# Expert part written out one expert ahead, shared part with its down projection inside the next chunk's gate-up

## The reference

```
attention:  pair[i,j] = relu(W2 relu(h_i - h_j + b1) + b2);  sim[i,j] = W3 pair[i,j] + b3, 0 on the diagonal
            for each token the 25 rows of largest sim, softmax over them in 32 heads of width 2, times Wout
mixture:    router -> 2 of 8 experts per token, capacity 1280 slots per expert
            expert:  h = silu(x Wgate) * (x Wup), width 176;  y = h Wdown
            shared:  the same shape on all tokens, width 704
```

## Time and profile before

| | us |
|---|---|
| three runs | 1804.5, 1806.66, 1807.19 (median 1806.66) |
| the profiled execution, own time | 1801.61 |
| its span in the profile | 1799.9 |
| stage 3, first gate-up to last down | 1325.0 to 1561.9 |
| stage 4, first product to the end | 1563.0 to 1799.9 |

### The profile page before, as it was taken

The page is one execution under the profiler, slowest core; times in us unless marked ns, Lnnn a source line. Parts: engine busy times, 40 slices in busy tenths (PEclk is TensorE's granted clock), DMA queues, the critical chain, the costliest instruction groups (busy, mean ns, idle before and its releaser), DMA issues.

```text
span 1799.9 us, 33525 instructions
## 1 busy us (share of the span) xinstructions
PE 1658.4 (92%) x9092; PEld 739.2 (41%) x9092; DVE 1514.7 (84%) x4279; ACT 1457.7 (81%) x2723; POOL 1121.8 (62%) x1045
## 2 busy tenths in 40 slices
PE   6989999999999999999999999999976878899897
PEld 5732222222222222222222222222246877877776
DVE  5876789999999999999999999999967675555555
ACT  4689999999999999999999999999965555423131
POOL 2203467777777777777777777776655501666564
PEclk9999999999999999999999999999988998999998
DMA  4511111121211212122111211111154533212131
GB/s 135 202 51 59 40 40 52 56 57 49 56 49 57 57 50 57 48 58 57 49 57 48 58 53 53 52 47 41 44 167 130 150 100 118 85 55 91 49 93 58
DMA packets 74726, 127.22 MB, mean 71 GB/s; under 512 B 21824, under 2 KB 43200, under 8 KB 74688
## 3 DMA queue, kind: packets, MB, share of 16 engines
q0 software_dynamic: 31744, 69.27, 14.0%
q1 hardware_dynamic: 42944, 57.53, 9.8%
HBM read 86.85 MB, written 35.65 MB: 68 GB/s over the span
## 4 chain that ended last, share of the span: by engine, by line
ACT 52%; issue 14%; PE 13%; DVE 10%; POOL 3%; DMA 1%; ACTq 1%; DVEq 0%; POOLq 0%
ACT arena L967 31%; ACT arena L980 18%; PE ps L809 7%; PE ps L768 4%; POOL arena L679 3%; ACT arena L984 1%; DVE hTe_low L1419 1%; DVE hTs_low L1488 1%; PE ps L779 1%; DMA arena<-slot_outputs,ysidx 1%; DVE xTe_low L1407 1%; DVE arena L1413 1%; ACT hTe_high L1051 1%; DVE arena L1326 1%; DVE arena L1256 1%
## 5 line engine op out<-in xcount | busy, mean ns | idle before, releaser
L615 POOL DMA_INDIRECT arena<-kv_rows,gidx x800 | 848.7, 1061 | 319.3 <-issue 226.3
L768 PE MATMUL ps<-arena,w2t 128*64 128x512 f32 x4096 | 946.8, 600 | 21.9 <-ACT arena L980 8.3
L967 ACT ACTIVATE arena<-arena 128x256 f32<-128x256 f32 x1696 | 804.7, 651 | 1.9 <-DVE arena L1246 1.9
L1256 DVE TENSOR_SCALAR arena<-arena 128x256 f32<-128x256 f32 x2400 | 746.0, 370 | 23.0 <-PE ps L768 20.7
L980 ACT ACTIVATE arena<-ps,b 128x1024 f32<-128x1024 f32 x512 | 639.7, 1250 | 5.5 <-PE ps L768 5.4
L768 PEld LDWEIGHTS ps<-arena,w2t 128*64 128x64 f32 x4096 | 273.3, 136 | 682.8 <-issue 577.1
L779 PE MATMUL ps<-arena,w3win 128*32 128x512 f32 x2048 | 272.8, 605 | 10.5 <-DVE arena L1267 10.3
L1092 ACT ACTIVATE arena<-ps 128x512 f32<-128x512 f32 x40 | 24.0, 599 | 152.9 <-PE ps L809 152.9
L779 PEld LDWEIGHTS ps<-arena,w3win 128*32 128x32 f32 x2048 | 40.3, 108 | 220.0 <-issue 180.1
L601 POOL DMA_INDIRECT slot_inputs<-xstage,istage x64 | 76.1, 1189 | 87.3 <-issue 70.4
L809 PE MATMUL ps<-xTe_high,wug_high 128*112 128x256 f32 (+1 forms) x240 | 77.5, 323 | 54.3 <-DVE xTe_low L1407 54.2
(11 more groups left out here) (144 smaller groups left out, 2020.3 us busy)
## 6 DMA issues: line engine op xcount, KB each, us to landing
arena<-kv_rows,gidx POOLq DMA_INDIRECT x800
slot_inputs<-arena SPq DMA_DIRECT2D x16, 640.0 KB, 3.9
arena<-slot_inputs SPq DMA_DIRECT2D x40, 256.0 KB, 3.2
slot_outputs<-arena SPq DMA_DIRECT2D x40, 256.0 KB, 2.1
xn<-in_L_attn_x_dram SPq DMA_DIRECT2D x16, 256.0 KB, 2.9
xstage<-xn SPq DMA_DIRECT2D x16, 256.0 KB
arena<-in_L_attn_x_dram SPq DMA_DIRECT2D x8, 512.0 KB, 3.8
out_dram<-arena SPq DMA_DIRECT2D x8, 512.0 KB, 4.6
```

What stands on the lines that cost most here:

```text
L615: pool.indirect_dma_start(out=kvg[:, h, r, :], out_offset=None, in_=kv_dram, in_offset=bass.IndirectOffsetOnAxis(ap=gidx[:, h, r:r + 1], a ...
L768: last = nc.tensor.matmul(ps_l2(s)[v * G2:(v + 1) * G2, u, :], w2t[:, :], r1[:, s % R1, 4 * u + 2 * v:4 * u + 2 * v + 2, :], start=True, s ...
L967: last = nc.scalar.activation(r1[:, s % R1, k, :], hneg_now, ACT.Relu, bias=hb_now[:, at:at + 1])
L1256: row = nc.vector.tensor_scalar(r1[:, s % R1, k, :], hneg_now, hb_now[:, at:at + 1], 0.0, ALU.add, ALU.max)
```

## The change

- **Expert part written out.** All 40 groups stand one after the other on every engine, numbered g = 0 to 39. `AHEAD = 2`: transposing and splitting of the slots run two groups ahead, across pairs, with three buffers for their halves.
- **The start.** SP loads the first expert's weights and slots when batch 15 has been copied out of the arena, not at the pair loop's end. POOL splits expert 0 between the gathers of tile 28 and those of tile 29, in the last batch of the pair loop. Slots 0 and 1 are transposed ahead of the last `layer3`, into banks 7 and 4. The loads of expert 1 and of the shared weights follow.
- **Weights.** ACT makes the high halves of expert e (1 to 5) one group ahead of DVE's low halves. POOL splits experts 0, 6 and 7.
- **Left-over attention.** Its pieces are spread over groups 0 to 35 in eight steps instead of five for each tile; POOL paces the last gathers by `gu_done`.
- **Shared part.** Written out, 8 chunks. While PE makes gate and up of chunk c, four down units of chunk c-1 follow each m. Two buffers for the tokens' halves, the activations' halves and the gathered outputs; the residual and the result keep one. The copies of queries and slot numbers (L674, L675) go. DVE weighs tiles 0 and 1 of chunk c-1 behind m = 3 and 4, tiles 2 and 3 behind the last m, and adds the residual in one instruction.

```diff
+    AHEAD = 2
-        xTe_r = [halves(f"xTe{i}", DC * 256, DC, 256) for i in range(2)]
+        xTe_r = [halves(f"xTe{i}", DC * 256, DC, 256) for i in range(AHEAD + 1)]
...
-        WEIGHTS_AT = {(0, 2): 1, (0, 8): 2, (1, 3): 3, (1, 8): 4, (2, 3): 5}
+        HIGH_AT = {2: 1, 7: 2, 12: 3, 17: 4, 22: 5}
+        LOW_AT = {3: 1, 8: 2, 13: 3, 18: 4, 23: 5}
+        ON_POOL = (0, 6, 7)
-        EXP_GROUP = {(0, 8): NT - 3, (1, 6): NT - 2, (2, 5): NT - 1}
+        EXP_GROUP = {11: NT - 3, 22: NT - 2, 31: NT - 1}
...
 # SP
-            sp.wait_ge(r1_dve, NB * BSTEPS)
-            sp.wait_ge(r1_act, NB * BSTEPS)
+            sp.wait_ge(batch_copied, 2 * NB)
...
 # POOL
                 for h in range(HALVES):
+                    if b == NB - 2 and h:
+                        wait_alone(pool, "pool", gathered[0], (b + 1) * (16 * TOPK))
+                        split_expert(0)
                     gather_tile(b, h, False, TOPK if b < NB - 2 else LAST_PACED[h] if b == NB - 2 else 0)
...
+            def gather_outputs(c):
+                if c >= 2:
+                    pool.wait_ge(comb_step, START + (c - 1) * CS)
+            def add_residual(c):
                 pool.wait_ge(resid_loaded, c * 16 + 16)
+            split_tokens(0)
+            split_tokens(1)
+            for c in range(NCH):
+                gather_outputs(c)
+                add_residual(c)
+                if c + 2 < NCH:
+                    split_tokens(c + 2)
...
 # PE
+            for g in range(AHEAD):
+                transpose_slots(g)
+            layer3(NB * BSTEPS, BSTEPS - 1)
+            for g in range(ALL):
+                if g + AHEAD < ALL:
+                    transpose_slots(g + AHEAD)
+                gate_up(g)
+                if g >= BEHIND:
+                    down(g - BEHIND)
...
+            for c in range(NCH):
+                for m in range(SM):
+                    if m == JC:
+                        transpose_heads(c)
+                    shared_gate_up(c, m)
+                    if c:
+                        shared_down(c - 1, UNITS[CT * m:CT * (m + 1)])
+            shared_down(NCH - 1, UNITS)
...
 # DVE
+            def expert_group(g):
+                if g + AHEAD < ALL:
+                    slots_low(g + AHEAD)
+                gate_times_up(g)
+                activations_low(g)
+                if g in LOW_AT:
+                    weights_low(LOW_AT[g])
+                if g in TOPK_AT:
+                    last_topk(*TOPK_AT[g])
+                if g in ATTENTION_AT:
+                    last_attention(*ATTENTION_AT[g])
...
+            OUTPUT_AT = {3: 0, 4: 1}
                     if m:
                         low(m - 1)
+                    if c and m in OUTPUT_AT:
+                        for k in range(2):
+                            weigh_output(c - 1, OUTPUT_AT[m], k)
                 low(JC)
+                if c:
+                    for n in range(2, CT):
+                        for k in range(2):
+                            weigh_output(c - 1, n, k)
+                    add_resid(c - 1)
```

More of the change, by code:

```diff
@@ L379, in lsn_attention_moe_block @@
         GATHER_AT = 9
-        CS = 3 * CT
+        CS = 2 * CT + 1
+        SM = JC + 1
+        UNITS = [(n, m) for n in range(CT) for m in range(SM)]
         GROUPS = BSTEPS // 2
@@ L493, in load_weights, with load_slots, store_group @@
                   .then_inc(we_loaded, 16)
[L495 to L514, removed]
+            def load_slots(g):
+                sp.dma_start(xe[g % GPE], expert_rows(slot_dram, g)).then_inc(xe_loaded[g % GPE], 16)
+            def store_group(g):
+                sp.wait_ge(down_copied, g + 1)
+                sp.dma_start(expert_rows(yslot_dram, g), oute[g % 2]).then_inc(y_stored[g % 2], 16)
             load_weights(0)
@@ L851, in down @@
                         last = products(ps_down(g)[:, n, :], [h[rows, m, n * P:(n + 1) * P] for h in hTe_r[g % 2]],
-                                        [h[rows, m, :] for h in wdn_r[i]], m == 0, m == 1)
+                                        [h[rows, m, :] for h in wdn_r[i % 2]], m == 0, m == 1)
                 last.then_inc(down_done, 1)
-            def expert_pair(j, first):
-                transpose_slots(j, 0, first)
-                for g in range(GB):
-                    if g < GB - 1:
-                        transpose_slots(j, g + 1, first)
-                    gate_up(j, g, first)
-                    if not (first and g < BEHIND):
-                        down(j, g - BEHIND, first)
@@ new lines, in shared_gate_up @@
+            def shared_gate_up(c, m):
+                if m == 0:
+                    pe.wait_ge(xT_split, c * 2 + 2)
+                if m >= 2 and m < JC:
+                    pe.wait_ge(smul_done, c * SM + (m - 1))
+                elif c and m == JC:
+                    pe.wait_ge(smul_done, c * SM)
+                elif c:
+                    pe.wait_ge(smul_done, c * SM - (1 + m))
+                for bank, at in ((2 * (m % 2), m * P), (2 * (m % 2) + 1, (JC + m) * P)) if m < JC else ((5, 2 * JC * P),):
+                    for k in range(DC):
+                        last = products(ps[:, bank, :], [w[:, k, at:at + P] for w in swug_r], [x[:, k, :] for x in xT_r[c % 2]],
+                                        k == 0, k == DC - 1)
+                last.then_inc(sgu_done, 1)
@@ new lines, in transpose_heads, with shared_down @@
+            def transpose_heads(c):
+                wait_alone(pe, "pe", aoT_low, START + c)
+                for n in range(CT):
+                    last = nc.tensor.transpose(ps[0:KD, 4, n * P:(n + 1) * P], qao[:, c * CT + n, :], ident[:, :])
+                last.then_inc(aoT_done, 1)
+            def shared_down(c, units):
+                for n, m in units:
+                    if n == 0:
+                        pe.wait_ge(slow_done, c * SM + (m + 1))
+                    if n == 0 and m == JC:
+                        pe.wait_ge(aoT_low, START + c + 1)
+                    if c and m == 0 and n % 2 == 0:
+                        pe.wait_ge(comb_step, START + (c - 1) * CS + (2 * n + 3))
+                    last = products(ps[:, 6 + n // 2, (n % 2) * D:(n % 2 + 1) * D], [h[:, m, n * P:(n + 1) * P] for h in hTs_r[c % 2]],
+                                    [w[:, m, :] for w in swdn_r], m == 0, m == JC)
```

435 lines of the change are left out of this document (201 added, 234 removed).

## The result

| | before | after |
|---|---|---|
| median of the runs of one comparison | 1805.58 us (4 runs, 1803.63 to 1807.19) | 1757.41 us (4 runs, 1753.95 to 1758.3) |
| ratio, 95% interval | 1 | 0.973 [0.9713, 0.9748] |
| profiled execution, own time / span | 1801.61 / 1799.9 us | 1753.95 / 1752.2 us |
| PE busy, granted clock from the first shared product on | 208.6 of 236.9 us, 0.94 | 196.1 of 210.35 us, 0.97 |

Forecast: 1754. Measured: 1757.41, 48.2 us less than before where 52 were forecast.

A forecast was written before the change was run, and what follows sets the result against it. No engine is full in the two later stages; DVE's own work and waits bound the expert groups, PE's work and waits the shared part. +2 - 4.2 - 16.8 - 33.0 = -52.0 us, forecast 1754 us, range 1742 to 1766.

The forecast's parts named there:

- three waits at pair ends: Expert part: DVE's waits of 4.48, 4.17 and 3.70 us, with no gate-up made ahead; all 12.4 us should go.
- rival B: Shared part: DVE and POOL bound it, period 24.2 to 28 us; at 27, +20 us, 1774; chance 0.13.
- A: Expert part: only its start gains, DVE bounds the groups and other waits replace pair ends; 1771 us; chance 0.14.
- Rival D: PE's written-out code: instruction fetch can't keep up, so the kernel is slower, 1817 at 1.3 us per group or chunk; chance 0.04.
- Part 1: Pair loop's last batch: splitting expert 0 on POOL costs +2 us, bounds 0 to +5.
- Part 3: The forty expert groups: DVE's floor of 189.3 us stays, waits change; last low half 19.0 us earlier, -16.8 for the groups.
- Exponentials: Expert groups 11, 22 and 31: DVE waits for ACT behind its table changes, 10.4 us in all against 9.7 before.
- The hand-over: From the groups' last low half to the first shared product: forecast 0 change.
- So it is just hidden: End of the expert part: POOL's later shared split, 15.7 + 3.8 us, fits in some 24 us; cover 4 us.
- Part 4, chunk 0: Shared part's first chunk, without down products: 15.5 us.
- 4 us of slack per m: Shared part: multiply m is needed only for gate-up m + 2, 5.6 us later, so DVE may be 4 us late.
- Part 4, the tail: From the last gate-up to the end: +20.5 us, the single-buffered residual last, its POOL additions ending at +15.7.

The follow-up runs named there:

- e6: The changed kernel with two more copies and subtractions on POOL directly ahead of expert 0's split: 1760.73 us, ratio 0.976 to the kernel before.
- e7: The changed kernel with own last-chunk residual and result buffers, expert 5's weights one group earlier, chunk 0's residual additions held back: 1747.37 us, ratio 0.9678.
- e10: The same kernel as e7, run again in another comparison as partner of e8: 1747.56 us, ratio 0.9685 to the kernel before.
- e4: The changed kernel with separate buffers for the last chunk's residual and result: 1752.95 us, ratio 0.9718 to the kernel before.
- e5: The changed kernel with expert 5's weights' high and low halves one group earlier: 1752.82 us, ratio 0.9714 to the kernel before.
- e8: e7 with the first shared gate-up on PE ahead of the last group's down products: 1745.01 us, ratio 0.9671 to the kernel before.

## Why the prediction was right, and where its sizes were off

*Right by its steps.* The three waits at pair ends had one cause and went together. The period of chunks 1 to 7 was 24.16 against 24.2, at full clock; POOL's locks on DVE did not reach PE there. So rival B (period 27) is out, and by the groups' -18.9 so is A, which gave the expert part its start only. Rival D, the fetch of PE's written-out code, would have shown as gaps between products; the window of 145.00 busy us in 145.00 has none. The Trainium skill, Runtime: NRT & Kernel Launch, section Instruction fetch mechanics, has instructions fetched in sequence, ahead of use; that row agrees with it.

*Part 1, the split of expert 0: right, as far as one profile before can tell.* +1.7 from the common mark against +2. DVE's own rows there grew by 3.3 us (mark to its last row: 13.9 before, 17.2 after), and DVE's slack against PE took the rest. The Trainium skill, SBUF — State Buffer, section Who interferes with whom, gives the lock as exclusive. These rows, e6 and chunk 0 agree with it, for tensor_scalar, tensor_tensor and scalar_tensor_tensor on DVE. The section also says that issue order decides who blocks; chunk 0 does not show it so, since its low half of 3.48 us had begun 0.53 us before POOL's addition.

*Part 3, the groups: 2.1 too pessimistic.* Exponentials cost 9.7, not 10.4. The waits that I priced at 3.8 (the last four groups, and ACT's weights) are 0.3: xTe_low's 7.2 less the exponentials' 5.5 and the start's 1.4. POOL's locks cost 12.5 (3.4 beside experts 6 and 7, 9.1 in the last four groups) where I had 11. In those last groups I had added PE's bound to the lock, and they overlap. That makes 2.7 less, where 2.1 were measured; 0.6 I can't place.

*The hand-over: a term that I had at nothing, +1.0.* The last down products run at the lower clock (12 in 2.93 us) because PE had waited for the low halves that POOL held up. "So it is just hidden", on the shared split, was right for POOL and wrong for DVE and PE.

*Part 4, chunk 0: mis-sized by 4.4.* 15.5 was PE's work at full clock. 2.4 of the miss is the lower clock behind the same waits: the head transposes stand 16.1 us behind the first shared product, and the 60 products before them cost 13.7 at 0.229. 2.1 is DVE's low half beside POOL's addition: 24.8 us from the first to the second head transposes, 22.7 in e7 and e10. The "4 us of slack per m" needs down products between the gate-ups, and chunk 0 has none. There multiply m must be there one gate-up later, 2.7 us, of which silu and multiply take 1.6, so that 1.1 is left. PE's wait of 1.84 us was for multiply 4, behind which stand only the transposes and the half as long last gate-up, 1.8 us together, so that about 0.2 is left.

*Part 4, the tail: mis-sized by 2.0, and its cause named only in part.* The forecast let the residual be last, at +15.7. It was ready at +14.9, but DVE could not begin to weigh before chunk 6's store had landed (+11.4; "the residual's buffer is single" was said, the result's wasn't), and two weighings took 2.46 us beside POOL's addition. The last sum ended at +18.3 instead of +17.1, and store and end took 4.1 instead of 3.4. e4, with both buffers doubled, took 3.5 off. DVE then works without a pause from chunk 7's last multiply to its last sum; in e7 it waits once more, 1.0 us for PE's last down products.

Together: 4.4 + 2.0 + 1.0 too little, 2.1 + 0.8 + 0.2 too much, which makes the 4.3 us between -52.0 and -47.7.

## What to carry over

Price a stretch without its partner's work (the first chunk, the last) on its own: slack worked out for the steady state isn't there, and single buffers show only there. An operation that "just hides" on one engine has to be checked against the engine whose rows get longer beside it, and against what the clock does behind the wait. Before moving work into an engine's wait, ask whether other work of the bound engine can go there instead: e5 got about 3 us that way with one expert's two numbers changed, and e8 2.5 us with one reordering.

## What was not expected of the hardware

POOL's addition that starts 0.06 us behind DVE's low half costs it nothing; one that starts 0.16 us before its end makes 0.69 us into 3.48, though DVE had begun first. A weighing (scalar_tensor_tensor, 128x256) took 2.99 us in e4 beside POOL, 0.48 alone.

Not every DVE instruction is held up. In all these traces those with two tensors kept their time beside POOL when one of the two came from PSUM (the tile `ps`). Two weighings beside the same addition of POOL (1742.21 to 1744.61) in the kernel after:

```profile
1742.34 0.47 DVE L1518 SCALAR_TENSOR_TENSOR arena<-arena,route_w,ps 128x256 f32<-128x256 f32 x1
1742.84 2.06 DVE L1518 SCALAR_TENSOR_TENSOR arena<-arena,route_w 128x256 f32<-128x256 f32 x1
```

The multiply that reads `ps` likewise took 0.69 us at 1558.14, inside POOL's addition of 1556.94 to 1559.68.

On the clock: e8's PE stood still for 2.5 us until 1533.60, then worked without a pause, and the spacing of its products of 512 columns fell from 0.43 to 0.23 us at about 1539.8; its partner, with further waits of 0.81 and 0.73 us, was at 0.43 until 1546.5.
